# Message stage of a two-layer graph network: six periods of eleven pairs for eight of eight, and one PSUM bank for every small product

## The reference, cut to what matters

```
coef = w_comp[etype]                          # 4 numbers per edge
m = sum_b coef[:, b] * (h @ V[b])[src] * norm
agg = segment_sum(m, dst)
hn = relu(agg + h @ loop_w + bias)
y = hn @ ffn_w.T + ffn_b + h
out = (y - mean) / sqrt(var + 1e-8) * ln_g + ln_b      # then x + out, a second norm
alpha = q[dst] . k[src] / sqrt(C); softmax per dst; out = sum a * v[src]; relu; once more
```

## Time and profile before

| | us |
|---|---|
| median of 3 runs (lowest, highest) | 2104.95 (2104.41, 2105.17) |
| the profiled execution, its own time | 2104.61 |
| its span, first to last instruction | 2102.6 |
| PE busy in the span | 2020.3 (96%) |
| DVE, ACT, POOL busy | 1525.7, 1290.0, 701.7 |

### The profile page before, as it was taken

One profiled execution on the slowest core, in us unless ns is written; L12 is line 12 of the kernel. 1 busy time (PEld: TensorE's weight loads), 2 busy tenths in 40 slices (PEclk: granted clock), 3 DMA queues, 4 the chain that ended last, 5 costly groups with the idle time before them and its releaser, 6 DMA issues. The chain is left out here.

```text
span 2102.6 us, 53186 instructions
## 1 busy us (share of the span) xinstructions
PE 2020.3 (96%) x19165; PEld 1655.1 (79%) x19165; DVE 1525.7 (73%) x4191; ACT 1290.0 (61%) x2275; POOL 701.7 (33%) x802
## 2 busy tenths in 40 slices
PE   1899999999999999999997999999999999999998
PEld 1788888888888888888884777777777677777777
DVE  4877888788878887887835666666664676766675
ACT  1466666666666767666653666566664566566665
POOL 3667577657756765676400000000000000000000
PEclk9899999999999999999999999999999999999999
DMA  3011111111111111111113222222211222222220
GB/s 80 6 47 53 51 38 48 53 50 41 57 50 41 48 51 52 38 48 51 45 43 115 93 93 82 73 89 91 91 61 63 96 78 90 97 99 99 99 90 17
DMA packets 43018, 137.00 MB, mean 65 GB/s; under 512 B 9190, under 2 KB 24359, under 8 KB 36484
## 3 DMA queue, kind: packets, MB, share of 16 engines
q1 hardware_dynamic: 38484, 128.24, 16.9%
q0 software_dynamic: 4400, 6.80, 1.3%
HBM read 91.83 MB, written 43.20 MB: 64 GB/s over the span
## 5 line engine op out<-in xcount | busy, mean ns | idle before, releaser
L839 PE MATMUL ps<-matrixT,x_rows 125*128 125x256 f32 (+1 forms) x2500 | 579.8, 382 | 1.7 <-ACT aggT L930 1.7
L911 ACT COPY matrixT<-ps 125x500 f32<-125x500 f32 (+2 forms) x800 | 395.8, 583 | 200.5 <-PE ps L827 199.8
L839 PEld LDWEIGHTS ps<-matrixT,x_rows 125*128 125x128 f32 x2500 | 458.7, 190 | 68.9 <-issue 2.0
L1636 DVE CUSTOM_DVE_ANT_0 scores_l<-ps,bias_rows_l 125x500 f32<-125x500 f32 (+1 forms) x700 | 394.0, 619 | 43.1 <-issue 43.1
L1542 ACT COPY weightsT_l<-ps 125x500 f32<-125x500 f32 (+1 forms) x450 | 242.0, 539 | 298.6 <-PE ps L1459 298.2
L827 PE MATMUL ps<-high_weights,low_onehot 64*125 64x125 f32 x6300 | 404.6, 279 | 12.4 <-ACT matrixT L911 8.8
L827 PEld LDWEIGHTS ps<-high_weights,low_onehot 64*125 64x125 f32 x6300 | 366.8, 189 | 47.4 <-issue 29.6
L1459 PEld LDWEIGHTS ps<-eye,scores_l 125*125 125x125 f32 x2500 | 293.3, 189 | 125.3 <-issue 117.5
L1535 ACT ACTIVATE scores_l<-scores_l,neg_max_l 125x1500 f32<-125x1500 f32 x200 | 319.2, 1596 | 64.6 <-DVE neg_max_l L1670 64.5
L1459 PE MATMUL ps<-eye,scores_l 125*125 125x125 f32 x2500 | 336.4, 282 | 4.4 <-ACT weightsT_l L1542 2.4
L1445 PE MATMUL ps<-kT_l,q_tile_l 64*125 64x500 f32 (+1 forms) x1400 | 318.5, 567 | 6.6 <-DVE chunk_max_l L1636 4.8
(11 more groups left out here) (151 smaller groups left out, 1719.8 us busy)
## 6 DMA issues: line engine op xcount, KB each, us to landing
bias_rows_l<-bias SPq DMA_DIRECT2D x50, 1562.5 KB, 6.7
bias<-bias SPq DMA_DIRECT2D x75, 500.0 KB, 2.6
x_rows<-in_x SPq DMA_DIRECT2D x1, 1562.5 KB
bias<-bias SPq DMA_DIRECT2D x25, 62.5 KB
x<-x_rows SPq DMA_DIRECT2D x25, 62.5 KB
x_rows_l<-x SPq DMA_DIRECT2D x25, 62.5 KB
out<-rows_l SPq DMA_DIRECT2D x25, 62.5 KB
dst_int<-in_dst SPq DMA_DIRECT2D x1, 402.8 KB
```

Source lines behind the costliest of these rows:

```text
L839: last = nc.tensor.matmul(psG[:, BASES * SPLIT * side:BASES * (SPLIT * side + SIDE[side])], x[:, h, :], MT[side][:, 0:SIDE[side], BASES * ...
L911: last = nc.scalar.copy(MT[side][:, at:at + 2 * c - 1:2, 0:COLS], psP[bank][0:R, :].rearrange("p (i c) -> p i c", c=128)[:, 0:c, 0:COLS])
L1636: V.tensor_tensor_reduce(S[par][:, hd, lo:hi], psS[2 * ((par + j) % 2) + hd][0:R, 0:cw[j]], bias[par][0:R, lo:hi], 1.0, FLOOR, ALU.add, AL ...
```

## The change

- GROUP 8 to 11, PERIODS 8 to 6 (11, 11, 10, 11, 10, 10 pairs), BUFS 4 to 3. `sums` runs in three parts of 8, 8 and 9 chunks for four of 6, 6, 6, 7.
- `psP` has six banks, three groups of two (`FOURS`, four pairs each). PE waits for the copy of each group apart and signals each apart; ACT copies group by group.
- Turned counts, codes, digits, `acc`, y and the turned x all go to bank 7. Before each, PE waits until what stood there has been read. The counts go in runs of 8, 8, 5 and 4 chunks (in periods 0, 1, 2, 4), digits in period 2, codes in 3, `acc` in 4, y and x in 5.
- On ACT `counts_out` of side 0 moves into periods 3, 4, 5 (twice), that of side 1 into 0 and 1 (three times). On DVE `first` moves from the last period of step u+4 to period 1 of the next step; `second` from period 0 to 2, `third` from 6 to 4; `bias_row` comes behind `build_hot`.

```diff
-GROUP, PERIODS, BUFS, AHEAD = 8, 8, 4, 2
+GROUP, PERIODS, BUFS, AHEAD = 11, 6, 3, 2
+PAIR_AT = (0, 11, 22, 32, 43, 53, 63)
+FOURS = 3
 PIECES = 4
 RUN = 8
-RUN_AT = {1: 0, 3: 1, 5: 2, 6: 3}
+RUNS = (0, 8, 16, 21, T)
+RUN_AT = {0: 0, 1: 1, 2: 2, 4: 3}
 FAR = 1.0e28
-PARTS = (0, 6, 12, 18, T)
+PARTS = (0, 8, 16, T)
...
-LAST = PAIRS - GROUP * (PERIODS - 1)
 SPLIT = 64
 SIDE = (SPLIT, R - SPLIT)
-runs = [(RUN * i, min(RUN, T - RUN * i)) for i in range(PIECES)]
+runs = [(RUNS[i], RUNS[i + 1] - RUNS[i]) for i in range(PIECES)]
+HALF = FOURS * PERIODS // 2
...
-psP, psG, psT, psK = ps[0:4], ps[4], ps[5], ps[6]
-psM = ps[7]
-psD = psM[:, 128:256].bitcast(BF16).rearrange("p (c n) -> p c n", n=128)
-psC = psT[:, :].bitcast(BF16).rearrange("p (h n) -> p h n", n=128)
+psP, psG, psM = ps[0:6], ps[6], ps[7]
+psD = psM[:, 384:512].bitcast(BF16).rearrange("p (c n) -> p c n", n=128)
+psC = psM[:, :].bitcast(BF16).rearrange("p (h n) -> p h n", n=128)
+acc, psY, psX = psM[:, 256:256 + R], psM[0:R, 0:D], psM[:, 128:128 + R]
...
     def build_hot(s, par, k):
-        n, at, to = s * PERIODS + k, k % BUFS, slice(GROUP * k, GROUP * k + size(k))
+        n, at, to = s * PERIODS + k, k % BUFS, slice(PAIR_AT[k], PAIR_AT[k + 1])
         if k == 0:
             v.wait_ge(codesT_ok, s + 1)
         if not is_int(s) or n >= BUFS:
-            v.wait_ge(pairs_ok, n - (BUFS - 1))
...
     def first(u, par):
         v.wait_ge(lifted, u + 1)
+        if not is_int(u) or u >= 1:
+            v.wait_ge(x_t_ok, u)
         v.wait_ge(y_ps, u + 1)
...
         for k in range(PERIODS):
-            if k == 0 and inside(z):
+            if k == 1 and inside(z):
+                first(z, 1 - par)
+            if k == 2 and inside(z):
                 second(z, 1 - par)
-            if k == 6 and inside(z):
+            if k == 4 and inside(z):
                 third(z, 1 - par)
...
-            if k - 1 in RUN_AT and inside(u):
-                bias_row(u, RUN_AT[k - 1])
-            if k == 7 and inside(u):
-                first(u, par)
             if k < PERIODS - AHEAD and inside(w):
                 build_hot(w, 1 - par, k + AHEAD)
             if k >= PERIODS - AHEAD and inside(w + 1):
                 build_hot(w + 1, par, k + AHEAD - PERIODS)
+            if k - 1 in RUN_AT and inside(u):
+                bias_row(u, RUN_AT[k - 1])
...
+    def turn_digits(s, par):
+        pe.wait_ge(kinds_ok, s + 1)
+        for c in range(2):
+            last = nc.tensor.transpose(psD[:, c, :], digits[par][:, c, :, :].rearrange("p q n -> p (q n)"), eye16[:, :])
+        last.then_inc(digits_ps, 1)
+
...
+        for g in range(FOURS):
+            if n >= 1:
+                pe.wait_ge(evac_ok, (n - 1) * FOURS + g + 1)
+            for i in range(4 * g, min(4 * g + 4, size(k))):
+                for q in range(2):
+                    own = slice(SLOTS * q, SLOTS * (q + 1))
+                    last = nc.tensor.matmul(psP[2 * g + q][0:R, 128 * (i % 4):128 * (i % 4) + COLS], L[own, at, i, :],
+                                            Hw[own, at, i, 0:COLS], start=True, stop=True)
+            last.then_inc(pairs_ok, 1)
...
     def turn_counts(u, i):
         n, (g, k) = u * PIECES + i, runs[i]
-        pe.wait_ge(ctA_ok, n + 1)
-        pe.wait_ge(ctB_ok, n + 1)
-        if n >= 1:
-            pe.wait_ge(ln_ok, n)
+        pe.wait_ge(ctA_ok, u * PIECES + (g + k - 1) // 8 + 1)
+        pe.wait_ge(ctB_ok, u * PIECES + (g + k - 1) // 8 + 1)
         for h in range(g, g + k):
             last = nc.tensor.transpose(psC[0:R, h - g, 0:R], CT[:, h, :], eye16[0:R, 0:R])
         last.then_inc(c_ps, 1)
+
+    def read(u, i):
+
+        if inside(u):
+            pe.wait_ge(ln_ok, u * PIECES + i + 1)
...
+            if k >= PERIODS // 2 and inside(w):
+                sums(w, 0, k - PERIODS // 2)
+
+            if k == 0:
+                if inside(z):
+                    pe.wait_ge(y_ok, z + 1)
+                    if z >= 1:
+                        pe.wait_ge(x_t_ok, z)
                 if u == 0:
                     pe.wait_ge(turned_ok, len(TURNS) + 1)
-                acc = psM[:, 0:R]
-                nc.tensor.matmul(acc, loopw[:, :], xt[:, :], start=True, stop=False)
-                for b in range(BASES):
-                    last = nc.tensor.matmul(acc, V_b[:, b, :], aggT[:, b, :], start=False, stop=(b == BASES - 1))
-                last.then_inc(m_ps, 1)
-            if k == 5 and inside(w + 1):
+                if inside(u):
+                    turn_counts(u, 0)
+            if k == 1 and inside(u):
+                read(u, 0)
+                turn_counts(u, 1)
+            if k == 2:
+                read(u, 1)
+                if inside(u):
+                    turn_counts(u, 2)
+                if inside(w + 1):
+                    turn_digits(w + 1, par)
+            if k == 3 and inside(w + 1):
+                read(u, 2)
+                pe.wait_ge(digitsT_ok, w + 2)
                 turn_codes(w + 1, par)
-            if k == 6 and inside(u):
-                pe.wait_ge(h_ok, u + 1)
+            if k == 4:
+                read(u, 2)
                 if inside(w + 1):
                     pe.wait_ge(codesT_ok, w + 2)
-                nc.tensor.matmul(psM[0:R, 256:384], hT[:, :], ffnT[:, :], start=True, stop=True).then_inc(y_ps, 1)
-            if k == 7 and inside(z):
-                pe.wait_ge(y_ok, min(t - 3, T) if is_int(t) else t - 3)
-                if not is_int(z) or z >= 1:
-                    pe.wait_ge(x_t_ok, z)
+                if w == 0:
+                    turn_ffn(nc, pe, m, turned_ps, psM)
+                if inside(u):
+                    turn_counts(u, 3)
+                    pe.wait_ge(xt_ok, u + 1)
+                    pe.wait_ge(aggT_ok, u * 2 + 2)
+                    nc.tensor.matmul(acc, loopw[:, :], xt[:, :], start=True, stop=False)
+                    for b in range(BASES):
+                        last = nc.tensor.matmul(acc, V_b[:, b, :], aggT[:, b, :], start=False, stop=(b == BASES - 1))
+                    last.then_inc(m_ps, 1)
+            if k == 5 and inside(u):
+                read(u, 3)
+                pe.wait_ge(h_ok, u + 1)
+                nc.tensor.matmul(psY, hT[:, :], ffnT[:, :], start=True, stop=True).then_inc(y_ps, 1)
+            if k == 5 and inside(z):
                 pe.wait_ge(x_ok, z + 1)
-                nc.tensor.transpose(psM[:, 384:384 + R], xnew[1 - par][:, :], eye[0:R, 0:R]).then_inc(x_ps, 1)
+                nc.tensor.transpose(psX, xnew[1 - par][:, :], eye[0:R, 0:R]).then_inc(x_ps, 1)
     pipeline_loop(pe, step, AFTER, T)
 @block.scalar
...
+        if k in (0, PERIODS // 2) and (not is_int(w) or w >= 1):
             act.wait_ge(agg_ok, w * 2 - 1 + side)
             act.wait_ge((ctA_ok, ctB_ok)[side], w * PIECES)
-        for bank in range(4):
-            q, at, c = place(k, bank)
-            last = nc.scalar.copy(MT[side][:, at:at + 2 * c - 1:2, 0:COLS],
-                                  psP[bank][0:R, :].rearrange("p (i c) -> p i c", c=128)[:, 0:c, 0:COLS])
-        last.then_inc(evac_ok, 1)
+        for g in range(FOURS):
+            act.wait_ge(pairs_ok, n * FOURS + (g + 1))
+            for q in range(2):
+                at, c = place(k, g, q)
+                last = nc.scalar.copy(MT[side][:, at:at + 2 * c - 1:2, 0:COLS],
+                                      psP[2 * g + q][0:R, :].rearrange("p (i c) -> p i c", c=128)[:, 0:c, 0:COLS])
+            last.then_inc(evac_ok, 1)
...
     def counts_out(s, side, piece):
         lo, hi = 8 * piece, min(8 * piece + 8, T)
         if side == 0 and (not is_int(s) or s >= 1):
-            act.wait_ge(c_ps, s * PIECES - PIECES + piece + 1)
-        act.wait_ge(evac_ok, s * PERIODS + PERIODS // 2 * (side + 1))
...
         for k in range(PERIODS):
             if k == 0 and inside(u):
                 sums_out(u, 0)
-                counts_out(u, 0, 3)
+            if k == 3 and inside(u):
+                sums_out(u, 1)
+            if inside(w):
+                evacuate(w, k)
+            if k == 1 and inside(u):
+                nc.scalar.copy(xt[:, :], xT[:, bass.ds(u * R, R)]).then_inc(xt_ok, 1)
+            if k < 2 and inside(u):
+                counts_out(u, 1, k)
+            if k == 1 and inside(u):
+                counts_out(u, 1, 2)
+                counts_out(u, 1, 3)
+            if k == 3 and inside(w):
+                counts_out(w, 0, 0)
+            if k == 4 and inside(w):
+                counts_out(w, 0, 1)
+            if k == 5 and inside(w):
+                counts_out(w, 0, 2)
+
+            if k == 2 and inside(w + 1):
+                act.wait_ge(digits_ps, w + 2)
...
+            if k == 4 and is_int(w) and w == 0:
+                turned_ffn_out(nc, act, m, turned_ps, turned_ok, psM)
             if k == 4 and inside(u):
-                sums_out(u, 1)
-            if k == 5 and inside(u):
                 act.wait_ge(m_ps, u + 1)
                 if is_int(u) and u == 0:
```

(12 more changed lines are left out.)

## The result

| | before | now |
|---|---|---|
| median (lowest, highest), same chip, us | 2105.06 (2104.41, 2105.99) | 2082.09 (2081.69, 2082.76) |
| span of the profiled execution, us | 2102.6 | 2079.7 |
| PE, DVE, ACT, POOL busy, us | 2020.3, 1525.7, 1290.0, 701.7 | 1998.0, 1500.2, 1291.2, 706.6 |

The ratio is 0.9891, with a 95% interval of 0.9874 to 0.9908: 23 us faster, where 33 were forecast. The time lies inside the range (2059 to 2095) and outside the likeliest case's own (2060 to 2078).

What follows compares the result with a forecast made beforehand. PE's own work was taken to bound each message-stage step. Savings of 24 x 1.1 = 26 us in steps and 7 at the start gave 2104.6 - 26 - 7 = 2071.6, so 2072 as a median; range 2059 to 2095.

Steps and rivals of the forecast that it cites:

- the likeliest case: Whole kernel: shorter steps and an earlier start give 2072 us as a median, own range 2060 to 2078; chance 0.62.
- rival (a): ACT's standstill, once per two-step loop, falls into periods 0 or 1; PE loses 7 to 22 us, 2079 to 2094; chance 0.13.
- (b): POOL's loop mildly bounds the steps: build before `first` slowed, loop 41.2 us, 0.8 above PE, time 2087; chance 0.12.
- The waits within a run: PE's 12 bank-group waits a step inside the runs: cost taken as zero, upper bound 2.9 us.
- Fewer changes of kind: PE in 24 message-stage steps: fewer switches between pairs and sums save 1.1 us a step, 26 us in all.
- The change to sums: PE going from pairs to sums: six a step for eight, 0.24 us each, 0.48 saved.
- The direct returns: PE going from sums straight back to pairs: none a step for two, 0.30 us each, 0.60 saved.
- The start: Before the first full step: refill waits go, DVE's builds bound it; full steps begin at 89 for 96.06, 7 us gained.
- The drain: End of the message stage: its chain of sums, count turnings, dense layer and two norms keeps its links; zero gain.
- ACT's margins: ACT's gatherings for the first and second turned counts finish 0.8 and 0.6 us before PE needs them.
- POOL's loop: Coefs, gathers, landing, `slot_kinds`, build, `first` and root take 39.5 us a round against PE's 40.4, hidden by 0.9.
- (c): Coefs stretched by a tenth on top of a slowed build: POOL's loop 43.0 us, slower at 2131; chance 0.06.

Runs made afterwards that it cites:

- the kernel with one wait: The changed kernel with PE waiting once per period for all three bank groups to be emptied, instead of once per group: 2082.02 us, ratio 0.9892.
- eight periods: The changed kernel with eight periods of eight pairs, four buffers and four-part sums again, small products moved along, one bank and split waits kept: 2102.97 us, ratio 0.999.
- the kernel with the later codes: The changed kernel with only the second tile's codes taken in period 4 instead of 3 of the first step with pairs, on PE and ACT: 2076.49 us.
- ten copies: The changed kernel with ten extra unread 125-column copies on ACT in each step, ahead of the copy of xT in period 1: 2111.09 us, ratio 1.0028.

## Why the prediction was right, and where its sizes were off

The time alone would not tell the likeliest case from rival (a), whose 2079 to 2094 it also fits; the range reached so high for (a) and (b), and neither of them is what happened. The mechanism is told by the steps: of the signs named, the run of 44 loads came true (2.48 for 2.4), and the step didn't go above 41, though 40.69 is outside the 40.2 to 40.6. The first full step came at 93.83 and not near 89. Steps and start gave 12.0 us less than forecast (7.2 and 4.8), and the drain 1.7 that was not forecast.

**The waits within a run** (zero): right, shown by the kernel with one wait.

**Fewer changes of kind** (1.1 us a step, measured 0.785): the mechanism was right, since eight periods give back 41.47, and both terms were too large. In the mean over the stage, from start to start of the weight loads, all pairs of a step fell from 15.33 to 14.93, all sums from 20.85 to 20.46, the small products from 5.30 to 5.29.
- The change to sums, 2 x 0.24: measured 0.40 in all, 0.20 each. The 0.24 set the pairs' 1.94 for 32 loads against 0.053 a load of another line. The pairs' own rows now show the slope: in the mean 2.598 for 44 loads, 2.379 for 40, 1.943 for 32 and 1.724 for 28, so 0.0546 a load and 0.20 fixed.
- The direct returns, 2 x 0.30: measured 0.39 in all. The 0.30 is real, but the sums that stay cost more than 2.37 / 12 each. On side 1 12 loads take 2.37, 16 take 3.20 and 18 take 3.61: 0.206 for each load beyond the twelfth, where I priced 0.197. A run's first loads are cheaper by 12 x 0.206 - 2.37 = 0.10 together, and on side 0 (2.48, 3.35 and 3.78) by 0.11. There is one run fewer on each side, so both are lost once: 0.60 - 0.21 = 0.39. Why they are cheaper no run here tells.

The sum 0.40 + 0.39 is the 0.785 measured; over 24 steps the steps gave 18.8 us for the 26 forecast. The Trainium skill ("TensorEngine Tiling (Array Packing)", Tiling Modes, Key Properties) says that changing the tiling mode drains TensorE. The pauses in the rows agree: they stand where pairs and sums meet, 0.30 us at a direct return.

**The start** (7 us, measured 2.2): two links of the chain failed. POOL's timeline, the first and the last row of these coefs:

```profile
57.77 1.16 POOL L578 TENSOR_TENSOR coef_parts<-kinds,comp 128x512 f32<-128x512 f32 x1 [8.03 <-DVE digits L688]
...
77.68 0.45 POOL L581 TENSOR_TENSOR codes<-coef_parts 128x128 f32<-128x128 f32 x1
```

They began near the 58.3 forecast but took until 78.13, 20.4 us for 18.3; so codes were turned at 78.25 and not at 76.6. From there to the first full step I counted 12 us and it took 15.6. Of these 3.6 us the pairs took 1.9: the timetable implied a pause before the codes (builds for period 3 ready near 68, codes at 76.6), but not its consequence, that the pairs behind the 4.97 us ran at the clock's lower level and took 4.20 us for 2.26. The other 1.7 were not counted: the small products took 1.5 us for 0.2, and the return from the last sums was direct (93.83 - 89.75 = 4.1 for 3.7). The pause itself was avoidable, by 5.6 us in all, as the kernel with the later codes shows. Why coefs got longer is not settled. It isn't that DVE pauses less beside them: in the kernel before it was busy for 17.90 of the 18.04 us of the same coefs, now for 19.38 of 20.36. In the kernel with eight periods, which has builds of eight pairs, they took 18.04 at the start as well and 17.4 in later steps, for 20.4 and 19.0 with builds of ten and eleven. So they go with the longer periods and builds, and not with the one bank; which part of that does it was not tested.

**The drain** (zero, measured 1.7): the links are the same, their lengths are not. From the turned x to the last sums are 1070.60 - 1069.34 = 1.3 us for 1092.47 - 1090.34 = 2.1, as ACT has only one chunk's counts to gather ahead of the copy of the sums. From there to the dense layer nothing is gained (13.1 for 13.0). From the dense layer to y are 1086.08 - 1083.67 = 2.4 us for 1108.60 - 1105.46 = 3.1: before y now stands the logarithm of four chunks' counts and not of eight. The last norms give 0.2. The kernel with eight periods has the same drain, so it comes from the new order and not from the periods; which move on ACT gave how much is read from the order, not tested.

**ACT's margins** (0.8 and 0.6): 0.9 and 0.7 in the trace, 0.75 for the second by ten copies. Right; rival (a) didn't come about, since all full steps are equal to 0.01 us.

**POOL's loop** (39.5, hidden by 0.9): 37.9, hidden by 2.8. The landing of the gathers was taken as 2.8 us from the first tile and is 1.5; coefs to gathers (29.4 against 29.2) and `slot_kinds` to coefs (7.3 against 7.2) came out right, the first with coefs longer (19.0 for 18.3) and what follows them shorter. So (b) and (c) were further off than their chances said. Their path was also wrong: a late loop reaches PE through `first` and the one bank, at the turned counts, before it does through the codes.

## What to carry to other kernels

When a change removes switches between two kinds of matmul, price both kinds by two run lengths of the same line: the fixed part of a run is what goes, and it was 0.20 us for either kind here, not the 0.24 and 0.30 that a single length and a foreign line suggest. A bank shared by small products joins engines that had nothing to do with each other: for each product ask who reads the last one, and what that reader stands behind. The pause of TensorE at this start was paid twice, once as the wait and once at the lower clock behind it; filling 4.97 us of it gave 5.6, and in a steady step the same reordering cost 1.05 each time.

## What the runs showed of the hardware

- A lone transposition of 125 columns between sums and half-array pairs doesn't take the place of the pause: 2.67 us became 2.72.
- The fixed part of a run of half-array pairs was 0.20 us, at 0.0546 us a load, over runs of 28, 32, 40 and 44 loads.
- Waits long satisfied within a run of matmuls cost nothing: 2.48 us for 44 loads with three waits and with one.
- After a pause of 4.97 us the granted clock was 0.52 over the next 5.35 us.
- Six additions of 125x128 on POOL, estimated at 3 us, lengthened its loop by 6.8 us in the step shown. The same six took between 2.7 and 5.9 us together, single ones from 0.45 to 1.8.
- The same 16 coefficient operations on POOL took 18.0 us at the start beside builds of eight pairs on DVE, and 20.4 beside builds of ten and eleven.
